# One attention and FFN block on one core: weights streamed in halves, attention in units of two steps

## The chip, the cores and the metric

The kernel runs on one core of a Trainium2 chip. The metric is the device time of one execution in microseconds; the engines are named as in the profile: PE (TensorE matmul), PEld (its weight load), DVE (VectorE), ACT (ScalarE), POOL (GpSimd) and SP (SyncE, here only a queue that issues DMAs).

## The reference

`x` has 8 batch rows of 512 tokens with 256 channels, all fp32. Each row is layer-normalised; the result feeds an attention and an FFN, and both are added to `x`.

```python
xn = _layernorm(x)                                   # (8, 512, 256)
q, k, v = xn @ Wq, xn @ Wk, xn @ Wv                  # 32 query heads, 8 key/value heads, D = 64
q, k = _rope(q, k)
scores = einsum('bgrtd,bgsd->bgrts', qg, k) / 8
allowed = (j <= i) & (i - j < 128)                   # causal, window of 128
out = softmax(where(allowed, scores, -inf)) @ v      # then @ Wo
x = fwht(inp * SU_ug) / 64                           # FFN on the same xn
h = silu((x @ W_gate.T) * s1) * ((x @ W_up.T) * s2)
ffn = (fwht(h * SU_dp) / 64) @ W_down.T * s3
return x0 + attention + ffn
```

## The kernel before

The two Hadamard transforms are folded into the FFN weights in a prologue, once. Then a loop over the 8 batch rows runs an FFN stage and an attention stage. A matmul whose operands must keep nearly fp32 precision is done as three f32r matmuls (`three`, L750): high by high, high by low, low by high parts. The weights of Q, K, V, gate, up and down are held on chip as such high and low parts; the output weight `wo_sb` is held in plain fp32, and so are the scores, the transposes, the mixing with the values and the output projection.

Attention goes over 32 steps: step n is key/value head g = n // 4 and query tile i = n % 4 of 128 tokens, with the 4 query heads of g side by side. Because the window is 128, a tile of queries sees its own tile of keys and the one before it, which together fill one 128 wide square: `fold` (L686) puts the scores of the previous tile where the own tile's are masked. Per step: PE computes the scores into S (L878, two buffers), DVE folds (L693 or, for i = 0, L698) and takes the row maximum (L700), ACT does four exponentials with row sums (L493), DVE takes the reciprocal (L705) and scales the tile (L709), PE transposes the four squares into TR (L889), ACT copies them to `pt_sb` (L503), POOL cuts out the part of the own tile, `p_cur` (L409), and for i > 0 that of the previous tile, `p_prev` (L413), PE mixes both with the values into O (L906) and ACT copies the result to `o_t` (L508). The output projection of head group g (`project_out`, L911) adds into `acc` on DVE (L683).

Every engine runs its instructions in the written order and waits on semaphores. The order is by slot n, by hand. PE's slot n has the scores of step n, the transposes of step n - 2, the fillers of the slot (`fillers`, L81), and the mixing of step n - 3. Fillers are a Q or K projection, a V projection, half an output projection, or the transposing of the next row's input; a projection uses one of two PSUM banks in turn (`bank`, L774). DVE's slot n has the fold of step n, the normalising of step n - 1 and its part of the fillers (the two rotary products of a projection, L601 and L602, or the addition L683). POOL's slot n has the masks of step n - 2 and a rotary combination (`rotate`, L369). ACT's slot n has the copy of step n - 2, the exponentials of step n, the copy of O of step n - 3. SP issues the DMAs that rearrange rotated Q and K into `q_stack` and `k_stack`, four heads ahead at most, in a fixed queue.

Of the kernel before, what the change touches and what calls it, by code (L numbers as in the profile page):

```python
# [5 lines left out]
def attention_and_ffn_block(  # L6
# [55 lines left out]
    def job(kind, n):  # L62
# [9 lines left out]
    ROPE_SLOTS = {("q", 4, 0): (3, 4), ("k", 1, 0): (8, 9), ("q", 5, 0): (12, 13),  # L72
                  ("q", 6, 0): (16, 17), ("q", 7, 0): (20, 21), ("k", 0, NEXT): (28, 29)}
    NORM_SLOT = 24

# [5 lines left out]
    def fillers(b, n):  # L81

        found = []
        if 0 < n < TT - 1:
# [15 lines left out]
    for b in range(BATCH):  # L100
        for n in range(4):
            for j in HIDDEN_AFTER[n]:
                if n and j == HIDDEN_AFTER[n][0]:
                    USES += [("q", b, n, 0), ("gate", b, j, 0), ("q", b, n, 1), ("up", b, j, 0)]
                else:
                    USES += [("gate", b, j, 0), ("up", b, j, 0)]
        USES += [("v", b, 0, 0), ("v", b, 0, 1)]
        for n in range(LAST_SLOT + 1):
            USES += fillers(b, n)
        USES.append(("wo", b, NKV - 1, 1))  # L110
# [6 lines left out]

    def masks_upto(n):

        return 2 * (n + 1) - (n // TT + 1)  # L120

    MASKS = masks_upto(STEPS - 1)
# [6 lines left out]
    with ctx:  # L129
# [7 lines left out]
        wq_p = [sb(f"wq_{s}", [P, CT, NH * D], f32r) for s in ("hi", "lo")]  # L137
        wk_p = [sb(f"wk_{s}", [P, CT, NKV * D], f32r) for s in ("hi", "lo")]
        wv_p = [sb(f"wv_{s}", [P, CT, NKV * D], f32r) for s in ("hi", "lo")]
        wgu_p = [sb(f"wgu_{s}", [P, CT, 2 * F], f32r) for s in ("hi", "lo")]  # L140
        wd_hi = sb("wd_hi", [P, FT, C], f32r)
        wo_sb = sb("wo_sb", [P, NH * D // P, C])

        cos_sb = sb("cos_sb", [P, T])
        sin_sb = sb("sin_sb", [P, T])
# [19 lines left out]
        with ExitStack() as prologue:  # L165

            wq_stage = prologue.enter_context(nc.sbuf_tensor("wq_stage", [P, CT, NH * D], fp32))
            gu_stage = prologue.enter_context(nc.sbuf_tensor("gu_stage", [P, CT, 2 * F], fp32))
            down_stage = prologue.enter_context(nc.sbuf_tensor("down_stage", [P, FT * C], fp32))
# [3 lines left out]
        staging_rest = sb("staging_rest", [P, 1024])  # L173
        h_p = [[t[:, n, :] for n in range(2)] for t in (sb("h_hi", [P, 2, T], f32r), sb("h_lo", [P, 2, T], f32r))]
        wd_p = [wd_hi, sb("wd_lo", [P, FT, C], f32r)]
        ky = sb("ky", [P, 2, T])
# [5 lines left out]
        pt_sb = sb("pt_sb", [P, REP, P])  # L182
        p_cur = sb("p_cur", [P, 2, REP, P])
        p_prev = sb("p_prev", [P, 2, REP, P])
        o_t = sb("o_t", [P, REP // 2, T])
# [820 lines left out]
```

## Time and profile before

| | |
|---|---|
| three runs, median (lowest to highest) | 1468.56 us (1467.96 to 1469.19) |
| the profiled execution: its time, its span | 1469.15 us, 1467.4 us |
| PE, PEld busy | 1393.8 us (95%), 1019.3 us (69%) |
| DVE, ACT, POOL busy | 1065.0 us (73%), 764.6 us (52%), 604.7 us (41%) |
| granted clock of TensorE, mean | 0.994 |
| 16 DMA engines: q1's share | 18.6% |

A busy share says how long instructions of an engine were in flight. Matmuls overlap one another, so PE's cost is read from the start of one block of matmuls to the start of the next, in a timeline of PE. "Idle before" and the releaser behind it tell what an engine waited for. One batch row lasts 175.4 us (813.2 to 988.6 in the trace).

### The profile page before, as it was taken

What the parts mean: (1) busy time and instruction counts of PE and PEld (TensorE: products, weight loads), DVE (VectorE), ACT (ScalarE), POOL (GpSimd) and SP (SyncE); (2) the same over time, 40 slices, a digit from 0 to 9 for tenths busy, and PEclk for the clock granted to TensorE, in tenths of its full rate; (3) what the DMA queues carried; (4) which work ended last, traced back from release to release, by engine and by line L of the source; (5) the groups of instructions that cost most, each with busy time, mean ns of one, the idle gap of its engine ahead of it and who ended that gap; (6) DMA issues with size and microseconds to landing.
All of it is one profiled execution on the core that took longest, in us unless ns stands there. A gap on an engine that the chain in (4) does not pass through costs nothing. (4 is left out here: it accounts for less than half of the span.)

```text
span 1467.4 us, 32904 instructions
## 1 busy us (share of the span) xinstructions
PE 1393.8 (95%) x12264; PEld 1019.3 (69%) x12264; DVE 1065.0 (73%) x1770; ACT 764.6 (52%) x2806; POOL 604.7 (41%) x631
## 2 busy tenths in 40 slices
PE   5599999999999999999999999999999999999998
PEld 2386767767677676767668676786767767677675
DVE  5758885588846887468865788558884688846885
ACT  1336663466625566246652666436663466624665
POOL 3324543155431554235542354324543155431653
PEclk9799999999999999999999999999999999999999
DMA  8101212022020120202202121111212022120120
GB/s 295 36 22 45 55 34 58 15 60 52 23 73 23 45 53 14 73 22 56 56 15 58 41 49 45 37 36 45 56 34 59 14 58 52 23 58 23 45 58 25
DMA packets 51118, 71.17 MB, mean 49 GB/s; under 512 B 13072, under 2 KB 24848, under 8 KB 50448
## 3 DMA queue, kind: packets, MB, share of 16 engines
q1 hardware_dynamic: 49968, 68.34, 18.6%
q8 instruction: 99, 1.62, 0.5%
q10 hardware_dynamic: 992, 0.73, 0.2%
q14 instruction: 59, 0.48, 0.1%
HBM read 14.49 MB, written 4.19 MB: 13 GB/s over the span
## 5 line engine op out<-in xcount | busy, mean ns | idle before, releaser
L493 ACT ACTIVATE e_sb<-S,negmax 128x128 f32<-128x128 f32 x1024 | 362.2, 369 | 109.5 <-DVE negmax L700 109.3
L409 POOL TENSOR_SCALAR_AFFINE_SELECT p_cur<-pt_sb 128x512 f32<-128x512 f32 x256 | 185.9, 726 | 509.9 <-ACT pt_sb L503 461.1
L503 ACT ACTIVATE pt_sb<-TR 128x512 f32<-128x512 f32 x256 | 153.7, 600 | 196.0 <-PE TR L889 166.5
L918 PE MATMUL PROJ<-wo_sb,o_t 128*128 128x256 f32 x1024 | 244.7, 382 | 7.9 <-ACT o_t L508 7.8
L878 PEld LDWEIGHTS S<-k_stack,q_stack 64*64 64x64 f32 x5632 | 169.2, 132 | 103.4 <-issue 73.7
L709 DVE TENSOR_TENSOR e_sb<-e_sb,rinv 128x512 f32<-128x512 f32 x256 | 232.1, 907 | 8.7
L878 PE MATMUL S<-k_stack,q_stack 64*64 64x64 f32 (+2 forms) x5632 | 210.7, 274 | 7.8 <-ACT e_sb L493 7.8
L493 ACT ACTIVATION_READ_ACCUMULATOR e_sb<-S,negmax 128x1 f32 x1024 | 212.1, 207 | 0.0
L918 PEld LDWEIGHTS PROJ<-wo_sb,o_t 128*128 128x128 f32 x1024 | 184.4, 190 | 37.3 <-issue 16.5
L413 POOL TENSOR_SCALAR_AFFINE_SELECT p_prev<-pt_sb 128x512 f32<-128x512 f32 x192 | 190.0, 990 | 0.0
L381 POOL TENSOR_TENSOR qy<-prod 128x512 f32<-128x512 f32 x64 | 82.2, 1284 | 260.5 <-DVE prod L602 235.0
L693 DVE COPY_PREDICATED S<-diagonal_key,S 128x512 f32<-128x512 int8 x192 | 133.3, 694 | 74.7 <-PE S L878 72.9
L700 DVE TENSOR_REDUCE negmax<-S 128x4 f32<-128x512 f32 x256 | 176.9, 691 | 8.8
L601 DVE TENSOR_TENSOR prod<-PROJ,cos_sb 128x512 f32<-128x512 f32 x160 | 109.4, 684 | 95.1 <-PE PROJ L754 94.2
L906 PE MATMUL O<-p_cur,v_sb 128*64 128x256 f32 x1024 | 167.0, 404 | 10.7 <-POOL p_cur L409 8.6
L889 PE MATMUL TR<-ident,e_sb 128*128 128x128 f32 x1024 | 167.6, 286 | 8.3 <-DVE e_sb L709 3.9
L488 ACT ACTIVATE pt_sb<-PROJ 128x512 f32<-128x512 f32 x64 | 38.3, 598 | 234.2 <-PE PROJ L754 234.2
L889 PEld LDWEIGHTS TR<-ident,e_sb 128*128 128x128 f32 x1024 | 107.1, 140 | 38.6 <-issue 17.2
L508 ACT ACTIVATE o_t<-O 128x256 f32<-128x256 f32 x256 | 100.1, 391 | 51.3 <-PE O L906 50.9
L752 PE MATMUL PROJ<-xt_hi,wq_hi 128*128 128x512 f32 x256 | 111.4, 435 | 15.9 <-DVE wq_lo L559 14.7
L683 DVE TENSOR_TENSOR acc<-PROJ,acc 128x512 f32<-128x512 f32 x128 | 87.2, 681 | 41.9 <-PE PROJ L918 41.4
L906 PEld LDWEIGHTS O<-p_cur,v_sb 128*64 128x64 f32 x1024 | 50.9, 134 | 95.6 <-issue 68.9
(89 smaller groups left out, 2283.1 us busy)
## 6 DMA issues: line engine op xcount, KB each, us to landing
q_stack<-qy SPq DMA_DIRECT2D x512, 64.0 KB, 2.0
k_stack<-ky SPq DMA_DIRECT2D x256, 64.0 KB, 2.0
x_in<-x SPq DMA_DIRECT2D x8, 512.0 KB, 4.2
out<-acc SPq DMA_DIRECT2D x8, 512.0 KB, 3.1
gu_stage<-w_gate_up SPq DMA_DIRECT2D x2, 1024.0 KB, 6.7
wq_stage<-wq SPq DMA_DIRECT2D x2, 1024.0 KB, 10.6
wo_sb<-wo SPq DMA_DIRECT2D x1, 2048.0 KB, 10.3
down_stage<-w_down SPq DMA_DIRECT2D x1, 1024.0 KB, 8.9
```

The lines of the kernel that those rows point to most:

```text
L409: nc.gpsimd.affine_select(out=p_cur[:, n % 2, :, :], in_=pt_sb[:, :, :], compare_op=ALU.is_ge, fill=0.0, base=0, pattern=[[0, REP], [1, P] ...
L413: nc.gpsimd.affine_select(out=p_prev[:, n % 2, :, :], in_=pt_sb[:, :, :], compare_op=ALU.is_gt, fill=0.0, base=0, pattern=[[0, REP], [-1, P]],
L493: last = nc.scalar.activation(e_sb[:, n % 2, r, :], s_heads(n, 1)[:, r, :], ACT.Exp, bias=negmax[:, n % 2, r:r + 1], accum_out=rowsum[:, n ...
L503: nc.scalar.activation(pt_sb[:, :, :], TR[:, :, :], ACT.Copy).then_inc(t_copied, 1)
L693: nc.vector.copy_predicated(own.rearrange("p r (a k) -> p r a k", a=2), diagonal_key[:, :, :].rearrange("p r (a k) -> p r a k", a=2), diagonal
L700: nc.vector.tensor_reduce(negmax[:, n % 2, :], own, axis=AX.X, op=ALU.max, negate=True).then_inc(max_done, 1)
L709: nc.vector.tensor_tensor(e, e, r, ALU.mult).then_inc(norm_done, 1)
L752: nc.tensor.matmul(dst, lhs[0], rhs[0], start=first, stop=False)
L878: last = nc.tensor.matmul(dst[:, at:at + (blocks - 1) * step + 1:step, :], q_stack[rows, g % 2, slot, i * P + a * HP:i * P + (a + 1) * HP] ...
L889: last = nc.tensor.transpose(TR[:, r, :], e_sb[:, n % 2, r, :], ident[:, :])
L906: last = nc.tensor.matmul(O[odd * D:(odd + 1) * D, 0:2 * P].rearrange("p (m q) -> p m q", m=2), v_sb[:, i - earlier, g * D:(g + 1) * D], p ...
L918: last = nc.tensor.matmul(dst[:, t * C:(t + 1) * C], o_t[:, m, tok:tok + P], wo_sb[:, 2 * g + m, :], start=m == 0, stop=m == 1)
```

## The change

- Step pairs. PE's even slot n computes the scores of steps n and n + 1, then transposes step n - 2, then the slot's fillers; the odd slot n + 1 transposes step n - 1, does its fillers, and mixes steps n - 4 and n - 3. An `O` bank holds both steps of a pair. The fillers move: Q and K projections to even slots, output projections to slots 7, 11, 15, ... (first half) and 9, 13, 17, ... (second half); both halves for the last head group go into the next row's FFN.
- DVE's even slot: fold n, reciprocal of n - 1, fold n + 1, low part of O of an earlier pair; its odd slot: reciprocal of n - 1. The scaling by the reciprocal goes to POOL, before the mask of its slot.
- One mask a step: `p_cur` only. Where there is a previous tile, PE mixes the whole unmasked `pt_sb` with the values of the previous tile, and `p_cur` with the difference of the two value tiles, `v_step`, which POOL computes 3 times a row. `pt_sb` and `p_cur` get four buffers.
- The output projection becomes three f32r matmuls for each fp32 one; O and `wo` are split in high and low parts, O's by ACT (128x512) and DVE (128x512, `o_low`) once a pair.
- The Q and output weights are no longer resident. A ring of two pieces each holds one head group's 512 KB (high and low); row 0 loads the raw weights, splits them (ACT and DVE) and SP stores the split pieces to DRAM, later rows load them from there, on SP's queue among the stacking DMAs.
- The two rotary products of a projection become one DVE instruction of 128x1024. In the prologue x is normalised without waiting for the constants, only the first Q piece is split ahead of the FFN weights, and the folding of the down weights goes behind the first four hidden blocks of row 0.

The core of the diff:

```diff
-    ROPE_SLOTS = {("q", 4, 0): (3, 4), ("k", 1, 0): (8, 9), ("q", 5, 0): (12, 13),
-                  ("q", 6, 0): (16, 17), ("q", 7, 0): (20, 21), ("k", 0, NEXT): (28, 29)}
+    ROPE_SLOTS = {("q", 4, 0): (2, 4), ("k", 1, 0): (6, 8), ("q", 5, 0): (10, 12),
+                  ("q", 6, 0): (14, 16), ("q", 7, 0): (18, 20), ("k", 0, NEXT): (28, 30)}
...
-        if n in (STEPS, STEPS + 1) and b + 1 < BATCH:
-            found.append(("q", b + 1, 0, n - STEPS))
-        if n >= TT + 2 and n % TT >= 2:
-
-            found.append(("wo", b, n // TT - 1, n % TT - 2))
+        if n in (STEPS + 1, STEPS + 2) and b + 1 < BATCH:
+            found.append(("q", b + 1, 0, n - STEPS - 1))
+        if n >= TT + 3 and n % TT == 3:
+            found.append(("wo", b, n // TT - 1, 0))
+        if n >= 2 * TT + 1 and n % TT == 1:
+            found.append(("wo", b, n // TT - 2, 1))
...
+            def load_wo(b, g):
+
+                w = b * NKV + g
+                if w >= 2:
+                    row, n = divmod(w - 2, NKV)
+                    wait_apart(sp, "sp", wo_added, (row + 1) * 2 * NKV + 2 * n + 2)
...
+                def normalise(n):
+                    wait_apart(pool, "pool", rinv_done, b * STEPS + n + 1)
+                    e = e_sb[:, n % 2, :, :]
+                    r = rinv[:, n % 2, :].rearrange("p (r o) -> p r o", o=1).to_broadcast([P, REP, P])
+                    nc.gpsimd.tensor_tensor(e, e, r, ALU.mult).then_inc(norm_done, 1)
...
                 for n in range(STEPS + 2):
+                    if 1 <= n <= STEPS:
+                        normalise(n - 1)
                     if n >= 2:
                         mask(n - 2)
+                    if n in (0, 2, 3):
+                        value_step(max(n, 1))
                     for kind, m, row in rope_jobs(b, n, 1):
                         rotate(row, kind, m)
...
-                for n in range(LAST_SLOT + 1):
-                    if n < STEPS:
-                        fold(n)
-                    if 1 <= n <= STEPS:
-                        normalise(n - 1)
+                for n in range(LAST_SLOT + 2):
+                    if n % 2 == 0:
+                        if n < STEPS:
+                            fold(n)
+                        if 1 <= n <= STEPS:
+                            inverse_sum(n - 1)
+                        if n < STEPS:
+                            fold(n + 1)
+                        if n >= 6:
+                            o_low(b, (n - 6) // 2)
+                    elif n < STEPS:
+                        inverse_sum(n - 1)
...
+            def project_out(row, g, part):
+                dst = bank("wo", row, g, part)
+
+                pe.wait_ge(o_split, (row * STEPS + TT * g) // 2 + part + 1)
...
+                    terms = [(v_sb[:, 0, :], p_cur)]
+                    if i:
+                        terms = [(v_sb[:, i - 1, :], pt_sb), (v_step[:, i - 1, :], p_cur)]
...
-                for n in range(LAST_SLOT + 1):
-                    if n < STEPS:
+                for n in range(LAST_SLOT + 2):
+                    if n % 2 == 0 and n < STEPS:
                         scores(n)
+                        scores(n + 1)
                     if 2 <= n <= STEPS + 1:
                         transposes(n - 2)
...
-                    if n >= 3:
-                        values_mixed(n - 3)
-                project_out(NKV - 1, 1)
+                    if n >= 5 and n % 2:
+                        values_mixed(n - 5)
+                        values_mixed(n - 4)
```

## Rows read from the trace of the kernel before

**Rows 1.** Stages of batch row 4: window, length, busy and count by engine, clock, DMA, GB/s

```profile
813.20:829.90 16.70, 15.22 (x189) 10.61 (x188) 14.09 (x25) 11.59 (x49) 3.67 (x5) 1.00 0.21 48
829.90:931.50 101.60, 99.82 (x1048) 70.61 (x1047) 88.20 (x149) 65.06 (x271) 55.18 (x59) 1.00 0.18 41
931.50:942.20 10.70, 9.94 (x57) 6.61 (x55) 3.73 (x6) 3.54 (x8) 4.94 (x6) 1.00 0.00 0
942.20:988.60 46.40, 46.18 (x242) 38.14 (x240) 23.34 (x39) 13.90 (x22) 10.01 (x7) 1.00 0.22 57
```

**Rows 2.** Timeline of PE, two attention steps: start, length, instruction, shape, count

```profile
823.35 0.65 PE L906 MATMUL O<-p_cur,v_sb 128*64 128x256 f32 x4
823.93 0.67 PE L878 MATMUL S<-k_stack,q_stack 64*64 64x64 f32 x16
824.53 0.66 PE L889 MATMUL TR<-ident,e_sb 128*128 128x128 f32 x4
824.94 0.48 PE L752 MATMUL PROJ<-xt_hi,wq_hi 128*128 128x512 f32 x1
...
826.51 0.65 PE L906 MATMUL O<-p_cur,v_sb 128*64 128x256 f32 x4
...
827.53 0.89 PE L878 MATMUL S<-k_stack,q_stack 64*64 64x128 f32 x24
828.35 0.66 PE L889 MATMUL TR<-ident,e_sb 128*128 128x128 f32 x4
```

**Rows 3.** Timeline of PE, half an output projection

```profile
847.86 0.66 PE L889 MATMUL TR<-ident,e_sb 128*128 128x128 f32 x4
848.35 1.89 PE L918 MATMUL PROJ<-wo_sb,o_t 128*128 128x256 f32 x8
850.17 0.65 PE L906 MATMUL O<-p_cur,v_sb 128*64 128x256 f32 x4
```

**Rows 4.** Timeline of PE, first and last of 12 f32r matmuls of 256 columns

```profile
801.52 0.28 PE L752 MATMUL S<-wd_hi,h_hi 128*128 128x256 f32 x1
...
802.82 0.28 PE L754 MATMUL S<-wd_hi,h_lo 128*128 128x256 f32 x1
```

**Rows 5.** Timeline of DVE beside rows 2: folds and the reciprocal behind one

```profile
824.76 0.75 DVE L698 COPY_PREDICATED_SCALAR S<-later_key,masked 128x512 f32 x1
...
828.60 0.70 DVE L693 COPY_PREDICATED S<-diagonal_key,S 128x512 f32<-128x512 int8 x1 [0.26 <-PE S L878]
...
829.94 0.17 DVE L705 RECIPROCAL rinv<-rowsum 128x4 f32<-128x4 f32 x1
```

**Rows 6.** Timeline, all engines: POOL released by DVE

```profile
847.17 0.67 DVE L602 TENSOR_TENSOR prod<-PROJ,sin_sb 128x512 f32<-128x512 f32 x1
...
848.03 1.27 POOL L381 TENSOR_TENSOR ky<-prod 128x512 f32<-128x512 f32 x1 [0.88 <-DVE prod L602]
```

**Rows 7.** Timeline, all engines: transposes released by the scaled tile

```profile
903.15 0.79 DVE L709 TENSOR_TENSOR e_sb<-e_sb,rinv 128x512 f32<-128x512 f32 x1
...
904.00 0.66 PE L889 MATMUL TR<-ident,e_sb 128*128 128x128 f32 x4 [0.19 <-DVE e_sb L709]
```

**Rows 8.** Groups by shape: busy us, mean ns of one, idle before and its releaser

```profile
L556 DVE TENSOR_TENSOR xt_lo<-PROJ,xt_hi 128x512 fp32r<-128x512 f32 x16 | 10.9, 686 | 4.8 <-ACT xt_hi L451 4.8
L413 POOL TENSOR_SCALAR_AFFINE_SELECT p_prev<-pt_sb 128x512 f32<-128x512 f32 x192 | 190.0, 990 | 0.0
L383 POOL TENSOR_TENSOR qy<-prod 128x512 f32<-128x512 f32 x64 | 94.4, 1475 | 0.0
```

**Rows 9.** Timeline of PE, first scores of row 4's attention

```profile
813.22 1.32 PE L878 MATMUL S<-k_stack,q_stack 64*64 64x64 f32 x40
...
817.11 0.88 PE L878 MATMUL S<-k_stack,q_stack 64*64 64x128 f32 x24 [0.97 <-ACT e_sb L493]
```

**Rows 10.** Timelines of DVE and PE in the prologue

```profile
48.34 4.49 DVE L559 SCALAR_TENSOR_TENSOR wq_lo<-wq_stage,wq_hi 128x2048 fp32r<-128x2048 f32 x2 [1.11 <-ACT wq_hi L469]
...
52.89 0.79 PE L752 MATMUL PROJ<-xt_hi,wq_hi 128*128 128x512 f32 x1 [14.74 <-DVE wq_lo L559]
```

More of the change, by code:

```diff
@@ L106, in attention_and_ffn_block @@
                     USES += [("gate", b, j, 0), ("up", b, j, 0)]
+                if b and not n:
+                    USES.append(("wo", b - 1, NKV - 1, j))
         USES += [("v", b, 0, 0), ("v", b, 0, 1)]
@@ L109, in attention_and_ffn_block @@
             USES += fillers(b, n)
-        USES.append(("wo", b, NKV - 1, 1))
+    USES += [("wo", BATCH - 1, NKV - 1, part) for part in range(2)]
     TURN = {what: u for u, what in enumerate(USES)}
@@ L336, in _ @@
                                  ).then_inc(x_loaded, 16)
-                stack_q(1)
                 stack_k(1)
+                for m in (2, 3):
+                    if not b:
+                        save_wq(m)
+                    load_wq(b, m + 2)
+                if not b:
+                    save_wq(4)
                 for n in range(2, NKV):
@@ L344, in _ @@
                         stack(n)
+                    if not b and n == 2:
+                        save_wo(0)
+                        save_wo(1)
+                        save_wq(5)
+                    if not b and n == 4:
+                        save_wq(6)
+                    if not b and n == 5:
+                        save_wq(7)
+                    if 3 <= n <= 4:
+                        load_wq(b, n + 3)
+                    if 5 <= n <= 6 and b + 1 < BATCH:
+                        load_wq(b + 1, n - 5)
+                    if n >= 3:
+                        if not b and n >= 5:
+                            save_wo(n - 3)
+                        load_wo(b, n - 1)
+                if not b:
+                    save_wo(5)
+                load_wo(b, 7)
+                if b + 1 < BATCH:
+                    if not b:
+                        save_wo(6)
+                    load_wo(b + 1, 0)
+                    if not b:
+                        save_wo(7)
+                    load_wo(b + 1, 1)
                 wait_apart(sp, "sp", wo_added, (b + 1) * 2 * NKV + 2 * NKV)
@@ L521, in _ @@
                 h_high(0)
+                if not b:
+                    for n in range(FT // 2):
+                        wd_high(n)
                 for n in range(1, 4):
                     hidden = HIDDEN_AFTER[n]
-                    if n == 3 and b + 1 < BATCH:
-                        deviation(b + 1)
                     for j in hidden:
@@ L745, in _ @@
                             products(row, kind, m, part)
-                wo_add(NKV - 1, 1)
+            o_low(BATCH - 1, STEPS // 2 - 1)
+            for part in range(2):
+                wo_add(BATCH - 1, NKV - 1, part)
         @block.tensor
@@ L788, in project @@
             def project(row, kind, n, part):
-                w = wq_p if kind == "q" else wk_p
-                col = (2 * n + part) * P
                 dst = bank(kind, row, n, part)
                 pe.wait_ge(xt_done, row * CT + CT)
+                if kind == "q":
+                    u = row * NKV + n
+                    w, col = [wq_ring[:, n % 2, a, :, :] for a in range(2)], part * P
+                    if not row:
+                        pe.wait_ge(wq_split, n + 1)
+                    else:
+                        pe.wait_ge(wq_loaded[n % 2], 16 * ((u - NKV) // 2 + 1))
+                else:
+                    w, col = wk_p, (2 * n + part) * P
                 for c in range(CT):
```

385 lines of the change are left out of this document (234 added, 151 removed).

## The prediction, made before the change was run

> **What bounds the kernel now.** I read the stages of one batch row first [rows 1]: in the long middle of attention PE is in flight 99.82 of 101.60 us, in the FFN 46.18 of 46.40, at the full clock, with DVE next at 88.20. So PE's order is the bound and its idle time is nearly nil; what a block costs is its start-to-start time, not its length. That is the second view, PE's timeline. From [rows 2]: 4 mixings and the change to scores 0.58 (823.35 to 823.93); scores of a step with i = 0, 0.60; of another step 0.82; transposes 0.41; a projection of six f32r matmuls 1.57; 8 mixings 1.02. From [rows 3]: transposes ahead of an output projection 0.49, the projection 1.82. Third, DVE's timeline beside it [rows 5], for how long after its scores each link of the softmax comes: today the scaled tile is needed a slot later, so it hides.
>
> **PE's own work.** An output half is now 12 f32r matmuls of 256 columns, 0.118 us apart as in the FFN [rows 4] (1.30 for 11 intervals), 1.41 us, and about 0.18 for going over to and from fp32, which a Q projection also has (1.57 against 6 of twice the columns, 1.41). So 1.59 for 1.82, and the transposes ahead 0.41 for 0.49: 0.31 saved, 16 times a row, 5.0 us. Pairing saves the changes of array tiling: 8 mixings are 4 pairs of 0.213, 0.85, so 0.16 of the 1.02 is the change, and scores to transposes has about 0.10. I take 0.3 saved for each of 16 pairs, 4.8 us (between 0.16 and 0.5). If PE stayed the bound, a row would lose nearly 10 us. The one mask changes nothing on PE: the same 8 mixings.
>
> **What is on the path instead.** Take a pair ("unit") that starts with the scores of even step n at 0. PE wants to transpose step n - 1 after two scores (0.72, which is 0.82 less the change, + 0.82), transposes (0.41) and a projection (1.57): at 3.5 us. But that tile must first be scaled, and its reciprocal stands on DVE behind fold n, which waits for the scores of this same unit:
> - fold n starts 1.07 after its scores [rows 2, 5] (827.53 to 828.60), 0.83 for i = 0 (823.93 to 824.76);
> - the reciprocal starts 1.34 later [rows 5] (828.60 to 829.94) and takes 0.17: 2.58;
> - POOL starts 0.19 after DVE's end and needs 1.27 [rows 6]: 4.04. This scaling with a broadcast operand isn't in the trace; its bounds are 0.69 (DVE's price for such a tile, L556) and 1.475 (L383, some of which ran beside DVE work on SBUF) [rows 8]; I take 1.27, since DVE only has PSUM work then;
> - PE follows 0.06 later [rows 7] (903.94 to 904.00): 4.1 instead of 3.5.
>
> Then comes the output half. It needs `o_low` of the pair just finished, which stands on DVE behind fold n + 1: reciprocal at 2.41, next fold at about 2.65, its end 1.34 later at 3.99, `o_low` 0.69 as L556 [rows 8], 4.68, and 0.06 to PE: 4.74. The transposes, 4.1 + 0.41 = 4.5, are earlier, so the DVE queue sets it. From there 1.59 for the projection and 0.85 + 1.02 for both mixings: a unit without i = 0 takes **8.2 us**. With i = 0 fold n is 0.24 earlier, reduced by its longer copy (0.06): 4.56 + 1.59 + 0.43 + 1.02 = **7.6 us**.
> The same two slots today, with one Q and one output filler: 0.82 + 0.82 + 0.41 + 0.49 + 1.57 + 1.82 + 1.02 + 1.02 = 7.97, and with i = 0 7.31. So each unit with a Q filler is 0.2 to 0.3 slower, although PE has less to do. Worse, units 22, 24 and 26 have no Q filler; today they are 1.4 us shorter, in the change the chain is the same.
>
> The sum of one row, from S of step 6:
> - middle: 7 units x 8.2 + 5 x 7.6 + unit 24 with the x transposes, whose second waits for DVE's scaling of x and the addition ahead of it, about 9.1: 104.5, against 101.6 [rows 1]: **+2.9**, though one output half fewer is in it;
> - start: step 2's scores wait for the exponentials of step 0, 3.89 after the first [rows 9]; of these about 1.6 are the exponentials, as fold and maximum end at 2.3. Now step 3's scores come right behind and wait for the exponentials of step 1 (3.9, 0.5 for a value copy, 1.6, so 5.8 with the rest). Scores, transposes, a V and a Q projection follow, to the transposes of step 1 at 10.0; behind their copy (1.2) ACT does the exponentials of step 3, so step 5's scores start at 12.8, step 2's transposes at 13.6, step 3's at 16.0 (a projection, and POOL behind a `v_step`), the first two mixings end at 18.0. With 0.4 for the first combination step 6 starts at 18.4 against 16.7 [rows 1]: **+1.7**;
> - tail: POOL has the 2.5 us rotary combination of the next row's K in slot 30, ahead of scaling steps 30 and 31: in unit 30 it runs from 6.0 (fold, `o_low`, product) to 8.5, scaling 30 to 9.8, a mask to 10.4, scaling 31 to 11.7. So the last transposes come at 11.8, 3.6 into unit 32. Behind them 0.4 transposes, two Q halves 3.0, an output half 1.4, mixings 1.44 + 1.87 and a change: 11.9 against 10.7: **+1.2**;
> - FFN: two output halves now stand there, 24 x 0.118 = **+2.8**. PSUM banks are free in time (0.7 us addition against 1.4 us of matmuls).
>
> Together +8.6 a row, 69 us in all; between +5 (no cost for the change into the projection, start and tail half as bad) and +12.
>
> **The other edits.** POOL loses 192 masks of 0.99 [rows 8] and gets 256 scalings of 1.27: with two masks about 4 us of work in a unit of 8, 6.5 with a combination. It then delays the next scaling by less than the chain's own wait, except in the tail as counted. `v_step` (3 x 1.27 a row) lies at the start and moves step 3's transposes by 0.4, counted. The merged rotary product shortens DVE off the path. Mask and copy buffers of four take ACT's wait for POOL away; that wait hid behind PE. ACT copies the late transposes of a unit (4.1 + 1.2) and does the exponentials behind them (1.6), to 6.9; the second scores of the next unit want them at 8.9: nothing, with 2 us of cover.
> The streamed weights put 16 loads of 512 KB a row on SP's queue. `load_wo` waits for `wo_added`, and behind it stand the Q and K stackings of the next head; they wait anyway for scores that come a unit later, and are used three units later, so nothing. If that cover failed, each group would wait some us.
> Prologue: x no longer waits for the constants and PE's wait of 14.74 for Q's split goes [rows 10], but DVE's folding of the FFN weights, which ended just ahead of that split at 48.3 [rows 10], is late next; the FFN can start near 46 instead of 61, at first on the lower clock, then PE pays the down folding and waits for its splitting inside row 0, and 11 pieces are split in row 0. I take **-2**, between -12 and +8.
>
> Sum: 1467.4 + 69 - 2 = 1534; the profiled execution is 1.75 above its span and 0.6 above the median: **1535 us**, 1500 to 1570 within this case.
>
> A rule speaks against the move to POOL, and the rows agree: the tile that DVE scales in 0.69 costs POOL 1.27. The Trainium skill (GPSIMD Engine Reference, Engine selection) says that elementwise work on a tile belongs on VectorE and that GpSimd is about twice slower with two inputs. By its ratio of 1.96 for an add the scaling would be an estimated 1.35, the tile 0.08 later, and the sum the same, as `o_low` comes last in a unit.
>
> **Rivals.**
> 1. *The chain hides and PE stays the bound* (as it would if reciprocals or `o_low` came earlier than I walk). Units 7.4 and 6.75, 1.4 less for the three without a Q filler: 89 in the middle instead of 104.5, and with start, tail and FFN as above -7 a row: about 1413 (1395 to 1440). For it: PE is the bound in every row of today's profile. Against: the order on DVE is explicit. Chance 0.14. Half of the stall gone, 1440 to 1500: 0.09.
> 2. *POOL is slower than its rotary work*: at 1.74 (DVE and POOL both on SBUF, the upper half of L383's mean) the transposes come at 4.6 and the output half at 5.0, +0.3 for 13 units, and the rotary combinations no longer hide (+0.5 for five): +6 a row, 1580. Against: beside the scalings DVE reads PSUM. Chance 0.08. It decides from 1.5 us a tile.
> 3. *Streaming doesn't hide*: a load waits at SP's head and the stackings come late, or 1 MB a unit slows them; 2 us for each of 7 head groups, +14 a row, 1645. Against: DMA is busy 0.18 to 0.21 [rows 1]. It decides when a load holds the queue over two units. Chance 0.04.
>
> **How the numbers follow.** Forecast 0.65. The range 1450 to 1580 holds it and most of the half case, and half of rival 2. 0.2% is 3 us, about what a measurement tells from no change. Faster: rival 1 and a third of the half case and prologue surprises, 0.19; same 0.02; slower 0.79.
>
> **What would show it.** Right: in the profile after, PE's timeline has in each unit a gap of about 0.6 before the second transposes, released by POOL `e_sb`, and 0.2 before the output half, released by DVE `o_lo`; units of 8.2 and 7.6; the units from 22 to 26 no shorter than others; about 2 us idle ahead of step 30's transposes; the FFN 49.2. Wrong: if transposes start 0.41 after the block before them, the chain hid; if scores wait for `q_stack`, rival 3.

## The result and the profile after

The changed kernel takes **1528.47 us** (median of 4 runs, 1525.64 to 1529.43) against 1468.88 of the kernel before beside it: ratio 1.0403, 95% interval 1.0385 to 1.0421. It is 4% slower. The prediction was 1535 us, 1450 to 1580. The profiled execution took 1525.64 us, 1.7 above its span.

From the page of the changed kernel: the span, the engines' busy time (share, instructions), and two groups.

```profile
span 1523.9 us, 34032 instructions
PE 1359.1 (89%) x12776; PEld 1041.1 (68%) x12776; DVE 901.9 (59%) x1496; ACT 736.3 (48%) x2685; POOL 683.1 (45%) x719
L492 POOL TENSOR_TENSOR e_sb<-e_sb,rinv 128x512 f32<-128x512 f32 x256 | 266.0, 1039 | 376.5 <-DVE rinv L834 212.9
L1056 PE MATMUL TR<-ident,e_sb 128*128 128x128 f32 x1024 | 168.7, 288 | 98.8 <-POOL e_sb L492 96.2
```

PE has less to do and is idle more. PE's largest wait is new: of the 99 us that it is idle before transposes, 96 end with POOL's scaled tile.

Stages of batch row 4 after the change, in the columns and the order of [rows 1] (start, middle, tail of attention, FFN):

```profile
842.40:860.00 17.60, 14.08 (x182) 10.43 (x181) 11.37 (x20) 11.78 (x52) 10.42 (x11) 1.00 0.20 46
860.00:962.80 102.80, 92.28 (x1090) 68.96 (x1088) 68.24 (x121) 62.56 (x255) 56.17 (x64) 1.00 0.33 91
962.80:974.10 11.30, 9.12 (x63) 6.34 (x61) 4.52 (x5) 2.40 (x5) 4.60 (x7) 1.00 0.13 46
974.10:1023.10 49.00, 48.94 (x266) 40.92 (x264) 24.47 (x35) 13.11 (x22) 11.98 (x9) 1.00 0.37 108
```

Against [rows 1] that is +0.9, +1.2, +0.6 and +2.6: 5.3 us more. In the middle PE's busy time fell from 99.82 to 92.28 us while the stage grew: the 7.5 us won and 1.2 more are idle time of PE.

A unit in that stage (steps 16 and 17; unit 16 for short, by its first step) and the head of the next. Timeline of PE of the changed kernel: start, length, instruction, in brackets the idle time before and its releaser.

```profile
884.05 1.32 PE L1045 MATMUL S<-k_stack,q_stack 64*64 64x64 f32 x40
...
885.71 0.48 PE L901 MATMUL PROJ<-xt_hi,wq_ring 128*128 128x512 f32 x1
...
887.73 0.66 PE L1056 MATMUL TR<-ident,e_sb 128*128 128x128 f32 x4 [0.36 <-POOL e_sb L492]
888.46 0.36 PE L901 MATMUL PROJ<-wo_ring,o_hi 128*128 128x256 f32 x1
...
890.05 0.65 PE L1075 MATMUL O<-p_cur,v_sb 128*64 128x256 f32 x4
...
891.49 1.22 PE L1045 MATMUL S<-k_stack,q_stack 64*64 64x128 f32 x36
...
893.21 0.66 PE L1056 MATMUL TR<-ident,e_sb 128*128 128x128 f32 x4 [0.16 <-POOL e_sb L492]
...
895.35 0.66 PE L1056 MATMUL TR<-ident,e_sb 128*128 128x128 f32 x4
```

DVE and POOL beside it:

```profile
884.88 0.75 DVE L827 COPY_PREDICATED_SCALAR S<-later_key,masked 128x512 f32 x1 [1.91 <-PE S L1045]
...
886.28 0.17 DVE L834 RECIPROCAL rinv<-rowsum 128x4 f32<-128x4 f32 x1
886.36 0.68 DVE L822 COPY_PREDICATED S<-diagonal_key,S 128x512 f32<-128x512 int8 x1
...
887.68 0.68 DVE L668 TENSOR_TENSOR o_lo<-O,o_hi 128x512 fp32r<-128x512 f32 x1
...
886.63 1.04 POOL L492 TENSOR_TENSOR e_sb<-e_sb,rinv 128x512 f32<-128x512 f32 x1 [3.11 <-ACT pt_sb L609]
```

This is the chain walked in the prediction: fold of step 16, reciprocal of step 15 behind it, POOL's scaling, transposes. These come 3.68 after the scores. `o_lo`, behind the fold of step 17, ends at 4.31 and lets the output half start at 4.41. The unit takes 7.44 us, and the next, without i = 0, 8.01; there the first transposes wait too, 0.16 us, and the second come at 3.86.

**Where the 56.5 us of span come from** (stage windows of both traces): attention of row 0 starts at 98.8 instead of 109.0 (-10.2); it takes 144.9 instead of 129.2 (+15.7); attention of rows 1 to 6 takes 131.5 to 135.8 each instead of 129.0 to 130.2 (+19.6 together); the FFNs of rows 1 to 7 take 49.0 to 49.5 instead of 46.5 each (+19.0); the last row's attention and the output +12.3.

Part of it is the clock. The changed kernel has a mean granted clock of 0.980, the one before 0.994; twice the shortfall is the time at 1.2 GHz, 61 us against 18. A stretch at 1.2 GHz is called a spell below. The windows of the changed kernel for row 0's attention and for one of the spells, in the columns of [rows 1]:

```profile
98.80:243.70 144.90, 123.74 (x1329) 92.60 (x1328) 91.50 (x157) 82.19 (x321) 71.42 (x80) 0.93 0.34 97
...
1479.30:1482.60 3.30, 3.30 (x17) 2.41 (x17) 0.69 (x1) 1.26 (x8) 1.11 (x2) 0.50 0.00 0
```

Row 0's attention stands at 0.93, where before it was at 1.00. PE around that spell, same kernel:

```profile
1477.88 0.66 PE L1056 MATMUL TR<-ident,e_sb 128*128 128x128 f32 x4 [1.77 <-POOL e_sb L492]
1478.62 0.36 PE L901 MATMUL PROJ<-wo_ring,o_hi 128*128 128x256 f32 x1
...
1480.92 1.12 PE L1075 MATMUL O<-p_cur,v_sb 128*64 128x256 f32 x4
```

PE waits 1.77 us for POOL, starts, and some 1.4 us later its clock is at the lower level for 3.3 us: the output half takes 2.30 (1478.62 to 1480.92) instead of 1.59, the mixings 2.29 instead of 1.45, so this wait costs another 1.6 us after it has ended. The rows say the same: from the start of one row's attention to the next, rows 1, 4, 5 and 6 take 180.6 to 181.0 us without a spell, row 3 with two 183.7, row 2 with three 185.2.

### The profile page after: what moved, and what is told of

The parts are those of the page before. It is cut to its first block, busy times and chain, and to the rows that moved or that the text cites. A ratio compares the mean times of both kernels' runs of the same rounds, so it can differ in the third digit from the quotient of the medians.

```text
span 1523.9 us, 34032 instructions
## 1 busy us (share of the span) xinstructions
PE 1359.1 (89%) x12776; PEld 1041.1 (68%) x12776; DVE 901.9 (59%) x1496; ACT 736.3 (48%) x2685; POOL 683.1 (45%) x719
## 4 chain that ended last, share of the span: by engine, by line
PE 67%; DVE 10%; POOL 9%; issue 7%; ACT 6%; DMA 0%; POOLq 0%; DVEq 0%
PE PROJ L901 13%; PE O L1075 12%; PE PROJ L903 11%; PE PROJ L902 11%; POOL e_sb L492 7%; PE TR L1056 7%; PE S L1045 7%; ACT e_sb L599 3%; DVE S L822 2%; DVE prod L713 2%; PE S L901 2%; ACT pt_sb L609 2%; PE S L902 2%; PE S L903 2%; POOL qy L470 1%
## 5 line engine op out<-in xcount | busy, mean ns | idle before, releaser
L492 POOL TENSOR_TENSOR e_sb<-e_sb,rinv 128x512 f32<-128x512 f32 x256 | 266.0, 1039 | 376.5 <-DVE rinv L834 212.9
L713 DVE TENSOR_TENSOR prod<-PROJ,rope_sb 128x1024 f32<-128x1024 f32 x160 | 195.1, 1220 | 125.4 <-PE PROJ L903 125.4
L1056 PE MATMUL TR<-ident,e_sb 128*128 128x128 f32 x1024 | 168.7, 288 | 98.8 <-POOL e_sb L492 96.2
L1045 PE MATMUL S<-k_stack,q_stack 64*64 64x128 f32 (+2 forms) x5632 | 189.2, 272 | 27.9 <-ACT e_sb L599 27.9
L614 ACT ACTIVATE o_hi<-O 128x512 fp32r<-128x512 f32 x128 | 76.9, 601 | 186.5 <-PE O L1075 185.7
L594 ACT ACTIVATE e_sb<-PROJ 128x512 f32<-128x512 f32 x64 | 38.3, 598 | 259.3 <-PE PROJ L903 259.3
L901 PE MATMUL PROJ<-wo_ring,o_hi 128*128 128x256 f32 x512 | 154.7, 302 | 7.6
L903 PE MATMUL PROJ<-wo_ring,o_lo 128*128 128x256 f32 x512 | 146.7, 287 | 0.0
L902 PE MATMUL PROJ<-wo_ring,o_hi 128*128 128x256 f32 x512 | 146.6, 286 | 0.0
L1075 PE MATMUL O<-pt_sb,v_sb 128*64 128x256 f32 x768 | 121.7, 396 | 1.5 <-DVE o_lo L668 1.5
L901 PEld LDWEIGHTS PROJ<-wo_ring,o_hi 128*128 128x128 f32 x512 | 99.2, 194 | 28.5 <-issue 27.5
L1075 PE MATMUL O<-p_cur,v_step 128*64 128x256 f32 x768 | 116.8, 383 | 0.0
```

The lines of the kernel that those rows point to most:

```text
L492: nc.gpsimd.tensor_tensor(e, e, r, ALU.mult).then_inc(norm_done, 1)
L713: nc.vector.tensor_tensor(prod[:, 2 * part:2 * part + 2, :], both, rope_sb[:, :, :], ALU.mult).then_inc(prod_done, 1)
L901: nc.tensor.matmul(dst, lhs[0], rhs[0], start=first, stop=False)
L902: nc.tensor.matmul(dst, lhs[0], rhs[1], start=False, stop=False)
L903: return nc.tensor.matmul(dst, lhs[1], rhs[0], start=False, stop=last)
L1045: last = nc.tensor.matmul(dst[:, at:at + (blocks - 1) * step + 1:step, :], q_stack[rows, g % 2, slot, i * P + a * HP:i * P + (a + 1) * HP] ...
```

## The experiments

All are edits to the changed kernel except `e9_before_pool_scaling`, which edits the kernel before. Times are medians of 4 runs, with the ratio to the kernel before, timed on the same chip (1469.0 to 1469.6), and its 95% interval. Changed: 1528.5, 1.0403 [1.0385, 1.0421].

**1. The reciprocal ahead of the fold.** DVE, even slots:

```diff
-                        if n < STEPS:
-                            fold(n)
                         if 1 <= n <= STEPS:
                             inverse_sum(n - 1)
                         if n < STEPS:
+                            fold(n)
                             fold(n + 1)
```

> The changed kernel with one line moved on DVE: the reciprocal of step n - 1 stands ahead of fold n, not behind it. Theory (two links on DVE's queue: the scaling's, and o_low behind fold n + 1, which comes last): the second transposes of a unit no longer wait for POOL, but the output half still waits for o_low, which comes only 0.1 us earlier (4.41 to about 4.3 in a unit with i = 0); 13 units x 0.1 and a little at start and tail, 1510 to 1520 us. Rival (the scaling chain alone is the stall, o_low has slack): the whole stall of 0.8 a unit goes and the three units without a Q filler shrink by 1.4 more: about 1410 us. Rival (the order on DVE has no part in it): 1528.

Measured 1523.3 (1521.2 to 1530.2), 1.0377 [1.0351, 1.0403]. The timelines of PE and DVE:

```profile
880.50 0.48 PE L900 MATMUL PROJ<-xt_hi,wq_ring 128*128 128x512 f32 x1
...
881.99 0.60 PE L1055 MATMUL TR<-ident,e_sb 128*128 128x128 f32 x4
883.18 0.36 PE L900 MATMUL PROJ<-wo_ring,o_hi 128*128 128x256 f32 x1 [0.59 <-issue]
...
882.40 0.68 DVE L668 TENSOR_TENSOR o_lo<-O,o_hi 128x512 fp32r<-128x512 f32 x1
```

The second transposes no longer wait (1.49 after the projection began), but the output half stands 1.19 behind them instead of 0.73, until `o_lo` is done at 883.08. The first wait was real and its removal is worth next to nothing alone: 5 us, by intervals that overlap, so the timeline shows it better than the time does.

**2. `o_low` between the folds instead.** DVE, even slots; the reciprocal stays where the change has it:

```diff
                             inverse_sum(n - 1)
-                        if n < STEPS:
-                            fold(n + 1)
                         if n >= 6:
                             o_low(b, (n - 6) // 2)
+                        if n < STEPS:
+                            fold(n + 1)
```

> The changed kernel with o_low between the two folds and the reciprocal where it is, behind fold n. Theory: the output half starts 0.36 behind the second transposes, which still come at 3.7 (i = 0) for POOL's scaling: 0.37 less in 13 units a row, about 1485 to 1490 us. Rival (the scaling chain alone): no change, 1528. The two kernels with one move each tell how the stall divides: if the theory holds their gains don't add up to that of both moves.

Measured 1503.2 (1496.5 to 1504.4), 1.0223 [1.0199, 1.0246], 13 us above what was expected. The output half follows its transposes at 0.41, the transposes still come at 3.67: units of 7.1 and 7.75 instead of 7.4 and 8.05. So of the two waits `o_low` is the one that ends last, as walked. The reciprocal's ends before it and is still 0.5 us too late for PE, which in a unit with i = 0 is ready for the second transposes at 3.15 (experiment 1).

**3. Both.** The order of even slots is now reciprocal, fold n, `o_low`, fold n + 1.

> As the first, and o_low stands between fold n and fold n + 1. Theory: neither link is late, PE is the bound again: units of 7.2 (now 8.05) and 6.5 (now 7.43), the three without a Q filler 1.5 less still, so 15 us a row: about 1405 us, 1390 to 1430, below the kernel before (1468.9). Rival (the fillers of a unit or ACT's exponentials are late next, as the second fold comes 0.7 later): units stay above 7.5, 1460 to 1490. Rival (streamed weights cost the time): no gain beyond the first kernel's.

Measured 1493.0 (1492.0 to 1493.8), 1.0162 [1.0147, 1.0177]: a miss by 88 us. Units with i = 0 take 6.54, as expected; of the others, four in a row take 8.0 to 8.3 instead of 7.2, and the first 8.55. PE and POOL of this kernel:

```profile
860.59 1.55 PE L1045 MATMUL S<-k_stack,q_stack 64*64 64x128 f32 x48
863.15 0.66 PE L1056 MATMUL TR<-ident,e_sb 128*128 128x128 f32 x4 [1.01 <-POOL e_sb L492]
...
859.60 1.28 POOL L468 TENSOR_TENSOR ky<-prod 128x512 f32<-128x512 f32 x1 [2.21 <-DVE prod L713]
860.83 1.27 POOL L470 TENSOR_TENSOR ky<-prod 128x512 f32<-128x512 f32 x1
862.07 1.03 POOL L492 TENSOR_TENSOR e_sb<-e_sb,rinv 128x512 f32<-128x512 f32 x1
```

The rotary combination, 2.5 us in one piece, stands on POOL ahead of a scaling. In the changed kernel it was nearly covered: the first transposes behind a combination wait 0.2 us (0.16 above), and the unit's output half is later anyway. With the chain shortened the combination is next. The clock is 0.973, lower than in the changed kernel.

**4. The scaling back on DVE**, behind its reciprocal:

```diff
-                    if 1 <= n <= STEPS:
-                        normalise(n - 1)
...
                     nc.vector.reciprocal(rinv[:, n % 2, :], rowsum[:, n % 2, :]).then_inc(rinv_done, 1)
+                    dve.wait_ge(rinv_done, b * STEPS + n + 1)
+                    e = e_sb[:, n % 2, :, :]
+                    r = rinv[:, n % 2, :].rearrange("p (r o) -> p r o", o=1).to_broadcast([P, REP, P])
+                    nc.vector.tensor_tensor(e, e, r, ALU.mult).then_inc(norm_done, 1)
```

> The changed kernel with the scaling by the reciprocal back on DVE, right behind the reciprocal (0.69 us), POOL without it. Theory (the bound is DVE's queue in the first half of a unit): the transposes come in time at 3.2, but o_low stands 0.7 later and the output half with it: 13 x 0.7 a row less a little in the tail, 1580 to 1600 us, slower than the change. Rival (moving the scaling to the slower POOL is what cost the time): 1480 to 1510, faster than the change.

Measured 1599.4 (1597.4 to 1601.4), 1.0888 [1.0870, 1.0906], as expected. PE and DVE:

```profile
892.12 0.66 PE L1058 MATMUL TR<-ident,e_sb 128*128 128x128 f32 x4
894.09 0.35 PE L903 MATMUL PROJ<-wo_ring,o_hi 128*128 128x256 f32 x1 [1.32 <-issue]
...
891.05 1.02 DVE L836 TENSOR_TENSOR e_sb<-e_sb,rinv 128x512 f32<-128x512 f32 x1
891.99 0.68 DVE L820 COPY_PREDICATED S<-diagonal_key,S 128x512 f32<-128x512 int8 x1
...
893.31 0.68 DVE L666 TENSOR_TENSOR o_lo<-O,o_hi 128x512 fp32r<-128x512 f32 x1
```

Every microsecond put in DVE's queue ahead of `o_low` comes out of the output half (1.97 behind its transposes). In this order of work the move to POOL is a gain of 71 us, not the cause of the loss.

**5. The kernel before with its scaling on POOL.** The same four lines move to POOL's loop, ahead of the masks of the slot; nothing else changes.

> The kernel before with one part of the change: POOL scales by the reciprocal, in its slot ahead of the mask. Theory (POOL's 1.04 us does no harm where the transposes come a whole slot after the reciprocal): reciprocal 2.6 into the slot, scaled at 3.8, needed at 4.8: 1460 to 1480 us; POOL has 1.04 + 0.63 + 0.63 to 1.08 a step of 4, so only slots with a combination may be late. Rival (the scaling on POOL is slow wherever it stands): 1500 or more.

Measured 1502.9 (1499.6 to 1504.5), 1.0228 [1.0213, 1.0244]: the forecast of this run was missed by over 20 us. The steps of the middle keep the pitch of [rows 2] (scores 0.82, transposes 0.41, projection 1.58, mixings 1.01). Nearly all of the loss stands at each row's start: in row 4, 3.0 of 3.3 us are lost before step 7. Here the window at which the clock drops, and PE there:

```profile
851.80:855.20 3.40, 3.17 (x10) 2.72 (x11) 0.00 (x0) 1.96 (x9) 2.94 (x5) 0.50 0.02 5
```
```profile
848.37 0.88 PE L882 MATMUL S<-k_stack,q_stack 64*64 64x128 f32 x24
852.03 0.69 PE L893 MATMUL TR<-ident,e_sb 128*128 128x128 f32 x2 [2.78 <-POOL e_sb L422]
```

PE waits 2.8 us for a scaling behind the first combination of the attention stage (Q of head group 4), then runs at 1.2 GHz. That combination is itself late: POOL stood 1.35 us in front of it (848.49) until a DMA into `q_stack` had read the buffer that it writes. The combinations later in the row cost 0.3 us at most. So the move to POOL is free where each step's scaling has a slot of slack, and costs 34 us, lower clock included, where it meets a combination that comes late. It also shows what POOL gets back when DVE doesn't work on SBUF beside it: the masks `p_prev` take 0.64 us each instead of 0.99 [rows 8].

**6. No reloading of the streamed weights.** `load_wq` and `load_wo` return at once in rows 1 to 7 and PE's waits for them go; those rows read whatever pieces row 0 left in the rings.

```diff
+                if b:
+                    return
...
-                        pe.wait_ge(wq_loaded[n % 2], 16 * ((u - NKV) // 2 + 1))
...
-                    pe.wait_ge(wo_loaded[g % 2], 16 * (((row - 1) * NKV + g) // 2 + 1))
```

> The changed kernel, in which rows 1 to 7 don't reload the Q and output weights and use the pieces that row 0 left (so their projections are of other heads): no 512 KB loads and no waits for them on SP's queue or PE. Theory (the streaming is hidden): 1520 to 1530 us, as the change. Rival (streaming costs time, through SP's queue or the DMA engines): 1490 or less.

Measured 1533.7 (1530.1 to 1538.7), 1.0443 [1.0413, 1.0473]: 59 MB less through the queue (q1 moves 76.7 MB instead of 135.5) buys nothing. The time is 4 us above the expected range, with more spells (clock 0.974). The streaming is hidden.

**7 to 10. Moving the combination out of the way**, each on top of experiment 3. In 7 the whole combination runs a slot later:

```diff
-                    for kind, m, row in rope_jobs(b, n, 1):
+                    for kind, m, row in rope_jobs(b, n - 1, 1):
```

> Both DVE moves, and POOL does the rotary combination one slot later, behind the scaling of the odd slot. Open after the kernel with both moves (1493, expected 1405): its units with i = 0 are 6.5 as expected, but each unit behind a combination starts with 1.05 us idle ahead of the first transposes. Theory (POOL's combination of 2.5 us, which stands ahead of the scaling of step n, is what came late next): units without i = 0 fall from 8.3 to 7.2, five or six a row, 1445 to 1455 us. Rival (ACT's exponentials or the copies hold those transposes): units stay, 1493.

Measured 1485.8 (three of its four runs, 1485.4 to 1486.0), 1.0114 [1.0097, 1.0131], over 30 us above what was expected. Its profiled execution took 2572 us, for a reason not found, and isn't read; the trace of the next, which has the same edit, shows that the wait moved from the first transposes of a unit to the second, which come 0.9 late. In 8, besides, the next row's K is projected two slots earlier, ACT copies the values of slots 1 and 2 behind the exponentials of the slot, and POOL computes two `v_step` two slots later:

```diff
-                  ("q", 6, 0): (14, 16), ("q", 7, 0): (18, 20), ("k", 0, NEXT): (28, 30)}
+                  ("q", 6, 0): (14, 16), ("q", 7, 0): (18, 20), ("k", 0, NEXT): (26, 28)}
...
-                    if n in (0, 2, 3):
-                        value_step(max(n, 1))
+                    if n in (0, 4, 5):
+                        value_step(max(n - 2, 1))
```

> As the former, and the next row's K projection and combination two slots earlier (slots 26 and 28, so that it is out of the way of the last steps' scalings and fills a unit that has no Q filler), ACT copies the values of slots 1 and 2 behind the exponentials of the slot, and POOL computes the later two value differences in slots 4 and 5. Theory: the tail loses about 3 us of waits a row, unit 30 its 1.5 us projection, the start 0.5 to 1: 5 us a row less, 1405 to 1415 us. Rival (start and tail are bound by ACT's exponentials and by the chain from the last scores): 1440.

Measured 1478.7 (1477.9 to 1481.5), 1.0064 [1.0048, 1.0081], over 60 us above what was expected. In neither of the two places could the scalings of a unit carry 2.5 us in one piece. So 9 cuts it (without the edits of 8): the first product pair behind the mask of its slot, the second behind the mask of the next.

```diff
+                    for kind, m, row in rope_jobs(b, n - 1, 1):
+                        second_half(kind, m)
                     for kind, m, row in rope_jobs(b, n, 1):
-                        rotate(row, kind, m)
+                        rotate(row, kind, m, split=True)
```

> Both DVE moves (reciprocal first, o_low between the folds), and POOL's rotary combination cut in its two instructions of 1.27 us: the first behind the mask of its slot, the second behind the mask of the next. Open after two kernels: with the combination whole in front of the scaling of step n the first transposes of the next unit wait 1.05 us (1493), with it whole behind, the second transposes wait 0.9, and those of the units 22 and 30 2.4 (1486). Theory (each wait is the part of the 2.5 us that a unit of 7 us can't hide): halves hide both, units of 6.6 and 7.2 throughout, 1435 to 1455 us. Rival (POOL as a whole is too full in those units, or the lower clock after short waits eats the gain): 1470 to 1485.

Measured 1479.4 (1477.4 to 1481.4), 1.0072 [1.0057, 1.0087], a miss by over 20 us. POOL's timeline:

```profile
850.24 1.27 POOL L468 TENSOR_TENSOR ky<-prod 128x512 f32<-128x512 f32 x1 [2.20 <-DVE rinv L841]
851.47 1.04 POOL L497 TENSOR_TENSOR e_sb<-e_sb,rinv 128x512 f32<-128x512 f32 x1
...
853.07 1.29 POOL L475 TENSOR_TENSOR ky<-prod 128x512 f32<-128x512 f32 x1
854.33 1.03 POOL L497 TENSOR_TENSOR e_sb<-e_sb,rinv 128x512 f32<-128x512 f32 x1
```

The second half (853.07) still stands ahead of the unit's second scaling, which is the one that PE wants soonest: those transposes come 0.8 late, and the unit takes 8.05 instead of 7.2. And 10 adds to it the K slots of 8 and ACT's order, without the later `v_step`:

> As the former, with the next row's K projection in slots 26 and 28, and ACT's value copies of slots 1 and 2 behind the exponentials of their slot. Theory: 3 us a row less in the tail and about 0.5 at the start: 1405 to 1430 us, below the kernel before. Rival (the tail is the chain from the last scores alone): 1445.

Measured 1453.2 (1452.9 to 1453.8), 0.9894 [0.9877, 0.9910]: 1% less than the kernel before, and over 20 us above what was expected.

**11. The second half behind the second scaling.** As 10, with:

```diff
+                    for kind, m, row in rope_jobs(b, n - 2, 1):
+                        second_half(kind, m)
                     if n >= 2:
                         mask(n - 2)
...
-                    for kind, m, row in rope_jobs(b, n - 1, 1):
-                        second_half(kind, m)
```

> As the kernel at 1453 us, and the second half of POOL's combination stands behind the next scaling (slot n + 2), not ahead of it. Left there: in each unit behind a combination the second transposes wait 0.8 us for their scaling, and in units 22 and 30, without a Q filler, 2.2; unit 22's is followed by 3.4 us on the lower clock. Theory (that scaling waits for POOL's second half, 1.23 us, and nothing else): five waits of 0.8 and 1.2 in each of the two others go, 6 us a row, and the spell of lower clock with them: 1395 to 1415 us. Rival (the scaling waits for its reciprocal, which in a short unit comes from ACT's exponentials): 1440 to 1455.

Measured **1400.3** (1399.8 to 1400.7), **0.9528 [0.9514, 0.9542]**, as expected, and 8.4% less than the changed kernel. Its stages of row 4, two of its units on PE, and POOL in the first of them:

```profile
775.73:792.86 17.13, 14.02 (x182) 10.40 (x181) 11.26 (x20) 11.81 (x52) 10.46 (x11) 1.00 0.21 47
792.86:883.63 90.77, 88.10 (x1090) 69.62 (x1089) 67.42 (x121) 60.59 (x254) 58.33 (x67) 1.00 0.37 103
883.63:893.83 10.20, 8.96 (x62) 6.29 (x60) 4.53 (x5) 2.94 (x6) 2.43 (x4) 1.00 0.15 51
893.83:942.90 49.07, 49.00 (x266) 40.96 (x264) 24.43 (x35) 13.12 (x22) 12.03 (x9) 1.00 0.39 108
```
```profile
806.71 1.55 PE L1053 MATMUL S<-k_stack,q_stack 64*64 64x128 f32 x48
...
813.93 1.32 PE L1053 MATMUL S<-k_stack,q_stack 64*64 64x64 f32 x40
...
820.47 0.77 PE L1053 MATMUL S<-k_stack,q_stack 64*64 64x128 f32 x18
...
808.53 1.05 POOL L497 TENSOR_TENSOR e_sb<-e_sb,rinv 128x512 f32<-128x512 f32 x1
809.53 1.29 POOL L475 TENSOR_TENSOR ky<-prod 128x512 f32<-128x512 f32 x1
```

The scaling (808.53) now runs before the second half. These units take 7.22 and 6.54 with no wait in them, 88.10 of 90.77 us of the middle are PE's, and its clock is 0.996 over the span. One row is 167.2 against 175.4.

The sum of PE's waits for the scaled tile (waits view, TR released by POOL `e_sb`) falls along this path: 96.2 us changed, 76.1 in experiment 3, 63.7 in 9, 59.1 in 10, 19.1 in 11:

```profile
PE TR L1064 <- POOL e_sb L497: 19.1, 22, 1.4
```

It doesn't order the times of all: experiment 1 has 44.4 and loses it before the output half, and experiment 2 has 107.7 and is 25 us faster than the changed kernel, since what it took away was the wait for `o_low`.

**12. One more step**, the Q projection of head group 4 one slot earlier and its combination two, `("q", 4, 0): (1, 2)`, on top of 11.

> As the former, with the first projection after the Vs (Q of head group 4) in slots 1 and 2, where PE waits for the first exponentials. Theory (the start is bound by ACT's row of exponentials and copies; a filler there takes PE work out of a later slot that then waits itself): 0 to 1 us a row less, at most 8 us below the former. Rival (PE's idle time at the start is free for it): 1.4 a row, 11 us below.

Measured 1458.8 (1457.0 to 1461.0), 0.9931 [0.9914, 0.9947]: 58 us worse than 11, where at most 8 less was expected. POOL, and the window at which the clock is low there:

```profile
819.90 1.26 POOL L468 TENSOR_TENSOR qy<-prod 128x512 f32<-128x512 f32 x1 [6.15 <-DMA q_stack<-qy]
...
819.40:829.60 10.20, 5.69 (x36) 3.45 (x40) 0.36 (x2) 4.58 (x19) 9.52 (x10) 0.50 0.00 0
```

The combination needs the buffer that the stacking of head group 2 reads, and that stacking waits for scores of step 3. POOL stands 6.15 us in front of it with the scalings queued behind; PE waits 4.95 us, and from within that wait on its clock is at the lower level for 10.2 us, 5.69 of them busy.

## Why the prediction was right, step by step

**What bounds the kernel, and PE's own work: right.** In experiment 11, where little else is late (0.8 us of wait each in units 22 and 24), the middle takes 90.8 us; the units of 7.22 and 6.54 are 0.2 under the 7.4 and 6.75 that rival 1 had. The saving is there, and in the changed kernel it is hidden by the chain.

**The chain: right, and shown.** Walked for a unit with i = 0, that is 0.18 earlier than without (0.24 less 0.06): fold at 0.83, reciprocal at 2.23, transposes at 3.92, the output half at 4.56; measured 0.83, 2.23, 3.68 and 4.41. Units 7.6 and 8.2 were predicted, 7.4 and 8.05 are there. Experiment 1 takes away the first link alone and gains 5 us, experiment 2 the second and gains 25, 3 both and 35, so the ends of both are in the right order. The gaps named as signs are there, smaller: 0.36 before the second transposes with i = 0 (0.6 was forecast); without i = 0 a part of it, 0.16 to 0.2, stands before the first transposes, behind a combination, which the walk didn't have. That units without a Q filler would be no shorter was right as well: unit 22 takes 8.05.

**The price of the scaling on POOL: mis-sized.** I took 1.27, the price of two dense inputs; this one, in place and with a broadcast second input, costs 1.04 ([rows 6] has the dense one). This is the 0.24 by which the transposes are earlier. It lies inside the stated bounds of 0.69 and 1.475. Compared with DVE's 0.69 it is a ratio of 1.5 and for two dense inputs 1.84. The Trainium skill (GPSIMD Engine Reference, Engine selection) gives about 2 for two inputs; the trace agrees for dense ones and shows less for this tile. Its rule that such work belongs on VectorE doesn't hold for this order of work, by experiment 4: the slower engine with the free queue wins by 71 us. In the order of the kernel before it holds, by experiment 5.

**The stages: right sign, about 60% of the size.** Predicted for a row: start +1.7, middle +2.9, tail +1.2, FFN +2.8, sum +8.6. Measured in row 4: +0.9, +1.2, +0.6, +2.6, sum +5.3. The middle was 1.7 too long in the forecast, about 0.15 for each of 12 units. The POOL term doesn't do this, as by the prediction's own walk the output half waits for `o_low`, not for POOL. It is the handover on DVE: the fold of step n + 1 was taken to start 0.24 behind the start of the reciprocal and starts 0.08 behind it (886.28 and 886.36), and `o_low` comes that much earlier. Start and tail were walked with the same 1.27 for every scaling and combination in a row, and I put no number on what overlaps; the idle ahead of step 30's transposes was to be 2 us and is 1.3.

**What made up for it was not foreseen.** Eight rows of +5.3 are 42 us, and the prologue gave -10.2 where I took -2. The span grew by 56.5, so 24 us are from elsewhere: row 0, whose attention is 13.2 longer than row 4's (144.9 for 131.7), and the spells at 1.2 GHz outside the prologue, which cost about 1.6 us each. 61 us at the lower level, less 14 in the first 98.8 us (clock 0.93), are some 14 spells: about 22 us. The two overlap, since six of the spells, 20 us of low time, are in row 0: 13.2 and the other eight spells are about 26. In experiment 11 row 0's attention is at 1.00 and still 9.1 longer than row 4's (127.2 for 118.1); what of this is the splitting of 11 pieces there wasn't separated. So the total came within 0.5% partly by luck: a term too large and one left out cancel.

**The other edits.** Streaming: rival 3 had 0.04, and experiment 6 refutes it. That POOL's combination is hidden except in the tail was right for the changed kernel, apart from the 0.2 us above, but only as long as the chain was late; experiment 3 shows it costing 1 us in a unit behind a combination as soon as it isn't. That was the failing step of the expectation of experiment 3, and of my rival 1, which took PE's pitch to follow once reciprocal and `o_low` came early. Rival 1's time, 1413, can be had (1400), but the queues of three engines have to be mended for it, not one: experiments 1 to 3 mend DVE's, 9 and 11 POOL's, and the K slots with ACT's order the row's end and start. Rival 2 (POOL at 1.74 beside DVE) is refuted for the scalings: their mean is 1.04, and none in the changed kernel took over 1.05.

**Between 9, 10 and 11.** The 53 us between 10 and 11 are more than the 40 us by which the waits for the scaled tile fell. Row 4 is 7.0 us shorter (174.2 to 167.2); 1.5 of it is a spell that 11 doesn't have, and 5.5 are units in which the scaled tile came late. Behind a combination the second transposes start 4.16 into the unit in 10 and 3.40 in 11, 0.76 earlier, where the waits view counts a wait of 0.60, as it counts from the modelled end of the block before. The 26 us between 9 and 10 are 3.1 in row 4: -2.0 at the start and -3.0 at the end, where 9 has a spell each, and +1.9 in the middle, where 10 has K's projection and a spell. The low time outside the prologue falls from 56 to 22 us, which is worth an estimated 15 to 17 of the 26 us.

**What stays open.** That the start's part of it is ACT's order and the end's K's slots is argued from where they stand; no run has one without the other. Open too: whether the splits in row 0 set its extra 9 us, and why one execution of experiment 7 took 2572 us.

## What to carry to other kernels

When two steps are paired so that PE saves changes of form, walk every in-order queue between the pair's scores and their next consumer: here the position of a 0.2 us reciprocal and of a 0.7 us low part behind the next step's fold decided. A slower engine is worth its price where its queue is free at that moment, and long pieces on it are to be cut and put behind the piece that is wanted first. Mend the queues together: the two edits on DVE gave 5 and 25 us alone, all edits together 128.

## What the runs showed of the hardware

**Short waits can cost twice.** In the kernel before PE had the full clock in attention (1.00 in [rows 1]). In the changed kernel PE waits 1.2 to 2.2 us in several units of each row (those at its start, and 22 to 26), and beside such waits the granted clock falls to 1.2 GHz for some 3.4 us now and then, with PE busy all through the spell (3.30 of 3.30 above): 61 us of low time in the changed kernel, about 80 in experiment 3 (clock 0.973), 11 in experiment 11 (0.996), nearly all of it in the prologue. Not every such wait does it: rows 1, 4, 5 and 6 have the same ones without a spell, and the kernel before waits up to 2.1 us once a row at 1.00. Waits of 4.7 to 5.6 us in each row of experiment 12 gave spells of 10.2 to 13.7 us. The Trainium skill (TensorE: Matmul & The Clock Gate, A second HAM failure mode: psum-queue depth-cycling) tells of a bf16 kernel whose clock goes to and fro because PE is idle for short moments between groups of matmuls; the traces here agree in that, at waits of up to 2.2 us in the changed kernel, and put about 1.6 us on a spell of 3.4.

**The scaling is cheaper on POOL than its other two-input work**: 1.04 us for 128x512, in place and with the second input repeated along the row, 1.27 to 1.29 with two full inputs where DVE doesn't stretch them, in each POOL timeline above. Whether the repeated input does it isn't shown: the scaling also multiplies and writes over its input, where the others add or subtract into another tile.

**DVE and POOL stretch each other** where both work on SBUF. In experiment 4 DVE's scaling took 1.02 us at 891.05, under two POOL instructions, and 0.69 at 888.44, where POOL's product took 1.79 in its place instead of 1.27; in the kernel before DVE's mean was 0.91, and with the scaling gone from DVE the masks `p_prev` fell from 0.99 to 0.64 (experiment 5). This is a part of what the move to POOL saves.
